# Two causal attentions of a fused kernel: two tiles per elementwise instruction, doubled buffers, a query transpose in another PSUM bank

## The reference, cut to what matters

```
layer 0: q, k = elu(.) + 1;  S_t = S_{t-1} + k_t v_t^T;  z_t = z_{t-1} + k_t
         y_t = (q_t S_t) / (q_t . z_t + 1e-6);  x += gate * (y @ w_proj)
layer 1: q, k rotated (rope), decay folded into the tables
         o_t = q_t sum_{s<=t} k_s v_s^T;  y = group_norm(o) * w + b
         x += gate * ((silu(h Wg^T) * y) @ Wo^T)
```

## Time and profile before

| | |
|---|---|
| runs (us) | 1041.17, 1035.74, 1040.65; median 1040.65 |
| span of the profiled execution | 1034.5 us, 25463 instructions |
| its time around the span | not listed apart; the three runs are 1.2 to 6.7 us over the span |
| busy, share of the span | PE 83%, PEld 59%, DVE 83%, ACT 61%, POOL 71% |
| mean granted TensorE clock | 0.937 |
| layer 0's attention, first to last products | 48.7 to 294.7 us |
| layer 1's attention, first to last products | 391.6 to 663.0 us |

### The profile page before, as it was taken

How to read it: one execution, slowest core, us unless ns; L and a number is a source line. 1 busy time by engine, 2 the same in 40 slices (tenths; PEclk the granted TensorE clock), 3 DMA queues, 4 the chain that set the end, 5 groups by cost and what they waited for, 6 DMA issues and landing times. The chain is left out here.

```text
span 1034.5 us, 25463 instructions
## 1 busy us (share of the span) xinstructions
PE 855.4 (83%) x5240; PEld 612.9 (59%) x5240; DVE 859.7 (83%) x2837; ACT 629.3 (61%) x1652; POOL 736.5 (71%) x642
## 2 busy tenths in 40 slices
PE   5699999999969968989898989558888733999993
PEld 4466666666636745555555555335655533999993
DVE  5589999999977976989888889778899861899995
ACT  2655555555429946676767675467765203998992
POOL 4488888888854528999999999655598471355554
PEclk9899999999989979999999999969999755999997
DMA  9520000000000000000000000264567564544420
GB/s 247 172 63 1 0 0 0 0 0 0 1 4 1 1 0 1 11 21 10 20 10 20 10 20 10 59 162 108 167 208 214 185 223 125 151 132 133 134 64 21
DMA packets 64935, 70.11 MB, mean 68 GB/s; under 512 B 8965, under 2 KB 52178, under 8 KB 64740
## 3 DMA queue, kind: packets, MB, share of 16 engines
q1 hardware_dynamic: 50612, 47.20, 16.5%
q0 software_dynamic: 6368, 16.89, 4.8%
q10 hardware_dynamic: 7872, 5.08, 2.0%
HBM read 32.32 MB, written 24.50 MB: 55 GB/s over the span
## 5 line engine op out<-in xcount | busy, mean ns | idle before, releaser
L473 PE MATMUL a_pS<-a_kv,utri 128*128 128x360 f32 (+3 forms) x768 | 263.1, 479 | 17.6 <-POOL a_kv L464 7.2
L464 POOL TENSOR_TENSOR a_kv<-a_qk,a_vv 128x1152 f32<-128x1152 f32 (+1 forms) x128 | 263.9, 2063 | 13.3 <-DVE a_qk L438 13.3
L473 PEld LDWEIGHTS a_pS<-a_kv,utri 128*128 128x128 f32 x768 | 135.5, 190 | 98.8 <-issue 24.6
L569 POOL TENSOR_TENSOR a_tt<-a_tt 128x576 f32<-128x576 f32 (+1 forms) x128 | 156.7, 1225 | 48.2 <-DVE a_tt L553 44.3
L553 DVE TENSOR_TENSOR a_tt<-a_pS,a_qk 128x360 f32<-128x360 f32 (+3 forms) x384 | 180.8, 526 | 9.1 <-PE a_pS L473 6.3
L1950 POOL DMA_INDIRECT out_dram<-x_o,x_place x71 | 69.4, 977 | 75.9 <-DVE x_o L1937 71.4
L581 DVE TENSOR_REDUCE a_nd<-a_tt 128x144 f32<-128x720 f32 (+3 forms) x128 | 104.3, 815 | 0.0
L519 ACT ACTIVATE a_tt<-a_pI 128x144 f32<-128x144 f32 (+1 forms) x96 | 40.1, 417 | 105.3 <-PE a_pI L481 105.2
L512 PEld LDWEIGHTS a_pO<-wgate,a_yT 128*128 128x128 f32 x256 | 44.6, 192 | 75.7 <-issue 42.5
L1530 POOL DMA_INDIRECT ys<-m_S,m_dest x64 | 62.9, 984 | 33.5 <-issue 12.5
L512 PE MATMUL a_pO<-wgate,a_yT 128*128 (+1 forms) x256 | 54.5, 295 | 31.5 <-POOL a_yT L543 22.6
(11 more groups left out here) (299 smaller groups left out, 2187.5 us busy)
## 6 DMA issues: line engine op xcount, KB each, us to landing
x_yl<-ys SPq DMA_DIRECT2D x71, 193.5 KB, 2.5
X<-xs SPq DMA_DIRECT2D x16, 256.0 KB, 5.3
kx<-m_kc SPq DMA_DIRECT2D x64, 64.0 KB
ax<-m_pc SPq DMA_DIRECT2D x64, 64.0 KB
m_S<-X SPq DMA_DIRECT2D x16, 256.0 KB, 4.4
xs<-X SPq DMA_DIRECT2D x15, 256.0 KB
w<-in_L_ffn_W_dram SPq DMA_DIRECT2D x1, 2048.0 KB
m_S<-gw ACTq DMA_DIRECT2D x6, 256.0 KB, 3.2
```

The lines of the kernel that those rows point to most:

```text
L464: pool.tensor_tensor(kv[:, t % 2, :, :, :], kk.unsqueeze(2).to_broadcast([P, H, J, D]), vv[:, t, :, :].unsqueeze(3).to_broadcast([P, H, J, ...
L473: pe.matmul(pS[c][:, 0:(h1 - h0) * SC], K.utri[:, :], flat[:, h0 * SC:h1 * SC], start=True, stop=True).then_inc(u_done, 1)
L569: pool.tensor_tensor(tt[:, t % 2, :, :, D // 2:D], tt[:, t % 2, :, :, D // 2:D], tt[:, t % 2, :, :, 0:D // 2], ALU.add).then_inc(half_done, 1)
```

## The change

The following is done for a pair of tiles (2u, 2u+1) in one instruction: kv, rope add, halving, gate product, denominator, reciprocal, y, its copy, square, variance, square root, residual. The three products, the sums, the state, the values' copy, exp and vec_qk stay per tile. kv and tt have four tiles instead of two. The query transpose moves from bank pI to columns 384 to 511 of the query bank pQ. `sum`, `y` and the rest now lag by one, two, three pairs. ScalarE loads the square root's table right after the silu. VectorE's short steps stand between the three products. Cut to its core:

```diff
-        qk = sb("qk", [P, TPB, 2 * P])
+        qk = sb("qk", [P, 2, TPB, P])
-        kv = sb("kv", [P, 2, H, J, D])
-        tt = sb("tt", [P, 2, H, J, D + 1])
+        kv = sb("kv", [P, TPB, H, J, D])
+        tt = sb("tt", [P, TPB, H, J, D + 1])
...
 def pe_qkv:
                 wait(pe, v_ready, m)
                 wait(pe, qk_free, m)
+                wait(pe, qT_ready, 3 * b - 3 + t)
...
+        def pool_kv(pool, b, u):
+            n, t = 2 * b + u, 2 * u
+            pool.wait_ge(qk_ready, qk_count(b, t + 1))
+            pool.wait_ge(v_ready, 4 * b + t + 2)
+            wait(pool, u_done, 6 * (n - 1))
...
+        def pe_transpose_q(pe, b, t):
+            m = 4 * b + 4 + t - 1
+            if isinstance(b, int):
+                m = min(m, NT)
+            pe.wait_ge(v_ready, m)
+            pe.wait_ge(qk_ready, qk_count(b, t))
+            pe.wait_ge(qk_free, m)
+            wait(pe, qT_ready, 3 * b + t - 1)
+            pe.transpose(pQ[:, QT:QT + P], qk[:, 0, t, :], K.ident[:, :]).then_inc(q_T, 1)
...
 def act_qT:
             act.wait_ge(q_T, 3 * b + t)
+            if known(b, 1):
+                act.wait_ge(qkv_ps, 4 * b + 4 + t)
...
 def act_gate:
+            act.activation(gate[slot], pT[:, :], ACT.Silu).then_inc(gate_ready, 1)
+            act.preload_act_table_set("sqrt_and_others")
...
+        def pe_step(pe, b, u, first=False):
+            ta, tb = 2 * u, 2 * u + 1
+            cur, back, out = pair(b, u, 0), pair(b, u, -2), pair(b, u, -3)
+            if cur and not first:
+                pe_states(pe, b, ta)
+            if out:
+                pe_project(pe, *out)
+            if cur:
+                if ta > 0:
+                    pe_inter(pe, b, ta)
+                pe_state_sum(pe, b, ta)
+                pe_transpose_q(pe, b, ta + 1)
+                if known(b, 1):
+                    pe_qkv(pe, b + 1, ta)
+            if back:
+                pe_transpose_y(pe, back, b, u)
+            if cur:
+                if layer == 1 and u == 0 and known(b, 1):
+                    pe_gate(pe, b + 1)
+                pe_states(pe, b, tb)
+                pe_inter(pe, b, tb)
+                if tb < 3:
+                    pe_state_sum(pe, b, tb)
+                    pe_transpose_q(pe, b, tb + 1)
+                if known(b, 1):
+                    pe_qkv(pe, b + 1, tb)
+                if u == 1 and known(b, 2):
                     pe_transpose_x(pe, b + 2)
...
+        def vec_step(v, b, u):
+            ta, tb = 2 * u, 2 * u + 1
+            cur, last, out, done = pair(b, u, 0), pair(b, u, -1), pair(b, u, -3), pair(b, u, -4)
+            late = last and known(last[0], 1) and (last[0] + 1, 2 * last[1] + 1)
+            if cur:
+                vec_product(v, b, ta, 0)
+            if layer == 0 and done:
+                vec_stats(v, *done, 0)
+            if layer == 1 and late:
+                vec_qk(v, *late)
+            if cur:
+                vec_product(v, b, ta, 1)
+            if layer == 0 and late:
+                vec_qk(v, *late)
+            if out:
+                vec_residual(v, *out)
+            if cur:
+                vec_product(v, b, ta, 2)
+            if last:
+                vec_sum(v, last[0], 2 * last[1])
+            if cur:
+                vec_state(v, b, ta)
+            if last:
+                vec_sum(v, last[0], 2 * last[1] + 1)
+            if cur:
+                vec_product(v, b, tb, 0)
+            if layer == 0 and last:
+                vec_den(v, *last)
+            if cur:
+                vec_product(v, b, tb, 1)
+                if known(b, 1):
+                    vec_qk(v, b + 1, ta)
+            if last:
+                if layer == 0:
+                    vec_rec(v, *last)
+                else:
+                    vec_var(v, *last)
+            if layer == 0 and done:
+                vec_stats(v, *done, 1)
+            if cur:
+                vec_product(v, b, tb, 2)
+                if tb < 3:
+                    vec_state(v, b, tb)
+            if last:
                 if layer == 1:
...
+                    vec_rec(v, *last)
+                vec_y(v, *last)
...
+        def pool_step(pool, b, u, phase):
+            last, back, ahead = pair(b, u, -1), pair(b, u, -2), pair(b, u, 1)
+            if last:
+                pool_halve(pool, *last)
+            if ahead:
                 if layer == 1:
+                    pool_rope(pool, *ahead)
+                pool_kv(pool, *ahead)
+            if layer == 1 and back:
+                pool_gate(pool, *back, (phase - 1) % 3)
```

More of the change, by code:

```diff
@@ L298, in attention @@
     SC = D * J
+    NP = NT // 2
     heads = [(0, 6), (6, 11), (11, 16)]
@@ L515, in act_inter, with pe_project @@
+        def pe_project(pe, b, u):
+            n = 2 * b + u
+            pe.wait_ge(yT_ready, n + 1)
+            wait(pe, x_done, n)
+            pe.wait_ge(y_ready, min(n + 2, NP) if isinstance(b, int) else n + 2)
+            for k in range(2):
+                mm = pe.matmul(pO[:, k * P:(k + 1) * P], yT[:, k, :], tile(K.wgate[:, 0 if layer == 0 else 2, :, :], b),
+                               start=True, stop=True)
+            mm.then_inc(proj_ps, 1)
         def act_inter(act, b, t):
@@ L663, in act_batch @@
-        def act_batch(act, b, half, last=False, more=True):
-            for t in range(TPB):
-                if t == 0 and not last:
+        def pe_step(pe, b, u, first=False):
[25 more added lines that the diff above has]
+                if u == 1 and known(b, 2):
+                    pe_transpose_x(pe, b + 2)
@@ L673, in act_batch @@
-                if layer == 1 and near(b, t, -1):
-                    act_square(act, *near(b, t, -1))
-                if t < 3:
-                    act_qT(act, b, t + 1)
-                if near(b, t, -2):
-                    act_yT(act, *near(b, t, -2))
-                if layer == 5 and t == 3 and more:
-                    act_modulate(act, b + 2)
-                if layer == 1:
-                    if near(b, t, -1):
-                        act_sd(act, *near(b, t, -1))
-                    if t == 2 and not last:
-                        act_gate(act, b + 1, 1 - half)
@@ L713, in pool_batch @@
-        def pool_batch(pool, b, half, last=False):
-            for t in range(TPB):
-                if not (last and t == 3):
-                    pool_kv(pool, 4 * b + t + 1, (t + 1) % 4)
-                if layer == 1:
-                    if near(b, t, -3):
-                        pool_gate(pool, *near(b, t, -3), half if t == 3 else 1 - half)
-                    if near(b, t, 3):
-                        pool_rope(pool, *near(b, t, 3))
-                pool_halve(pool, b, t)
+                    act_normalise(act, b + 2, ta)
@@ new lines, in act_step @@
+                act_qT(act, b, ta + 1)
+                if known(b, 1):
+                    act_qkv(act, b + 1, ta)
+            if back:
+                act_yT(act, *back)
+            if layer == 1 and last:
+                act_square(act, *last)
+            if cur:
+                act_inter(act, b, tb)
+                if more:
+                    act_normalise(act, b + 2, tb)
+            if layer == 1 and last:
+                act_sd(act, *last)
+            if cur:
+                if tb < 3:
+                    act_qT(act, b, tb + 1)
+                if known(b, 1):
+                    act_qkv(act, b + 1, tb)
+                if layer == 1 and u == 0 and known(b, 1):
+                    act_gate(act, b + 1, (phase + 1) % 3)
```

398 lines of the change are left out of this document (179 added, 219 removed).

## The result

The changed kernel takes 1054.82 us (median of 4 runs, 1050.93 to 1055.68) against 1040.91 for the kernel before: a ratio of 1.0145 [1.0119, 1.0171], slower by 13.9 us where 28 less were forecast. The profiled execution took 1054.64 us around a span of 1052.8.

A forecast was written before the change was run, and what follows sets the result against it. DVE bounds layer 0 and POOL layer 1; after the change, bank pQ's ring (7.5 us a pair) and POOL (7.68). Layer 1's -22.8 and layer 0's -5 take the 1034.5 us span to 1006.7, median 1013, range 995 to 1031.

The forecast's parts named there:

- signs of being wrong: What would refute the forecast: layer 1's period over 7.9 us a pair with POOL idle, or layer 0's over 7.8.
- The ring through bank pQ: Loop in each pair: DVE's qk reads bank pQ, PE projects, next states, first product; forecast 7.5 us a pair.
- Layer 1's ring: The same loop through bank pQ in layer 1, put at 7.5 us a pair, under POOL's 7.68.
- The early table load at nothing: Layer 1, square root's table loaded after the silu: delay on ACT put at no cost, 0.7 us a batch if uncovered.
- Layer 1's total: POOL bounds layer 1 at 7.68 us a pair; 244.1 against 272.7 us, -28.6, or -22.8 with the drain.
- Rival A: Rival, chance 0.1: POOL's time goes with the elements alone, so merging saves no fixed part; 17.4 us come back, 1030.
- Layer 0's total: Layer 0 at 7.5 us a pair: 240.8 against 247.4 us, -6.6, or -5 with the drain.
- The drain of layer 1: Statistics after layer 1's last products come 5.8 us later (+3 to +7); bank pO waits for the last pair's y.
- Layer 0's fill: Layer 0's first product comes 2.9 us later, since the first kv covers two tiles.
- C: Rival, chance 0.1: query transpose and its ACT copy lengthen bank pQ turns; zero gain at 0.52 us a pair, 1058 at 0.8.
- D: Rival, chance 0.08: the early table load does not help, sd is late again; 11 us, giving 1024.
- B: Rival, chance 0.2: layer 0's bank pQ loop is shorter, POOL's ring or PE bounds at 7.2 or less; 1003 to 995.

The follow-up runs named there:

- run 7: Changed kernel with the residual behind the third product of the pair's first tile instead of ahead of it; 1048.6 us, ratio 1.009 to the kernel before.
- Run 6: Changed kernel with PE's gate matmul of layer 1 behind the second tile's states instead of ahead of them; 1047.5 us.
- run 3: Kernel before with only the early table load added, the square root's table loaded right after the silu; 1051.9 us, ratio 1.012.
- run 9: Run 1 with the other qk step (next batch's second tile) also moved ahead of the first tile's first product; 1018.7 us.
- run 10: Run 9 with a tile's three products in a row again and the short steps behind them; 1016.5 us.
- run 13: Run 1 with each layer's first kv in two instructions and the last pair's reciprocal in bank pQ, its residual order changed for the drain; 1014.4 us.
- run 5: Run 1 without the early table load behind the silu; 1032.3 us.
- run 11: Changed kernel with a tile's three products in a row, so each qk step stands behind all three; 1125.8 us.
- run 1: Changed kernel with qk of the next batch's first tile ahead of the second tile's first product instead of after its second; 1027.4 us.
- run 4: Changed kernel without the early table load; 1051.5 us, ratio 1.011 to the kernel before.
- run 8: Changed kernel with the first tile's qk moved half as far, ahead of the second tile's second product but behind its first; 1032.9 us.
- Run 2: Kernel before with only the query transpose moved to bank pQ, with the changed kernel's waits; 1039.2 us, ratio 0.999.
- run 12: Run 1 with each layer's first kv in two instructions, layer 1's reciprocal in SBUF and an earlier residual at the drain; 1025.0 us.

## Why the prediction was wrong

Both of its signs of being wrong came: layer 1's period over 7.9 with POOL idle, and layer 0's over 7.8.

**The ring through bank pQ** is the step that failed. The prediction drew it rightly ("The new tie is bank pQ") and put it at 7.5 us in both layers, where 8.0 and 8.5 were measured. In layer 0, in two consecutive pairs (the step that the prediction calls odd is the one shown above, the even one runs from 101.92 to 109.88):

| link | forecast odd, even | measured odd, even |
|---|---|---|
| step's start to the first tile's qk | 5.03, 5.18 | 5.30, 5.47 |
| qk to PE (transpose of q in even steps) | 0.48 | 0.51, 0.51 |
| PE until the states start | 1.08, 0.77 | 1.20, 1.06 |
| states' start to first product | 1.03 | 1.03, 0.92 |
| pair | 7.62, 7.46 | 8.04, 7.96 |

One piece has a name and comes in every pair: the residual's wait for the projection, 0.19 to 0.22, which I had left out as if pO were always ready; run 7 got 0.23 a pair for it. The rest are small pieces of up to 0.2, of which the projection is the one that comes in both steps: 0.72 and 0.75 us until the next instruction starts, 0.64 forecast. A sum of bare durations leaves such pieces out, and the ring came 7% over it.

**Layer 1's ring** was waved through with "the same, 7.5". It was 8.4 and 8.6. On it stand two waits that weren't counted, one in each pair of a batch. From the timeline of the changed kernel:

```profile
505.15 0.41 PE L521 MATMUL a_pI<-ident,a_y 128*128 128x128 f32 x2 [0.86 <-ACT a_tt L538]
506.24 1.03 DVE L574 TENSOR_TENSOR a_tt<-a_pS,a_qk 128x384 f32<-128x384 f32 x2 [0.74 <-PE a_pS L485]
...
513.17 1.02 PE L670 MATMUL a_pT<-a_hT,W 128*128 128x512 f32 x2
514.88 1.03 DVE L574 TENSOR_TENSOR a_tt<-a_pS,a_qk 128x384 f32<-128x384 f32 x2 [0.40 <-PE a_pS L485]
```

In one pair DVE waits 0.74 for the second tile's states, which stand behind the transpose of y and so behind the table loads; in the other it waits 0.40 for them behind the gate matmul (0.86 us, once a batch). Without these two waits both pairs, 8.71 and 8.38, would be at 7.98, as far over the forecast as layer 0's. Run 6 took the second away, 7.6 us or 0.5 a batch.

**The early table load at nothing** rested on a cover: "PE's last projection waits for a later DVE step anyway". That projection was not where the delay went. It went to the transpose of y and to the states behind it in PE's queue (0.81 us on ACT's copy in the changed kernel, 1.37 in run 3), ahead of the wait that was to hide it. The price named for a failed cover was 0.7 a batch. Run 3 lost 0.46 in a batch by the chain, and 0.8 on average over 15 with what came with the clock.

**Layer 1's total** (-29.7 for the products, -5.2 measured): with the rings out of the way (runs 9 and 10) POOL does set the period, as forecast, at 7.90 instead of 7.68. That term was mis-sized by 0.22, and not in the merges: the records shrank by 0.77 a pair, less four overlaps of 0.05, which is the forecast 0.56. What it left out is kv's new wait of 0.16 for the rope add, in place of an overlap of 0.05. Rival A did not come: the fixed part was the instruction's. The prediction had read the Trainium skill (Advanced Engine Details and Errata, The Read-Write Bubble) as saying that nothing would be saved. That page says only that the bubble between instructions doesn't affect GpSimd; a fixed part inside the instruction, as in the 7.85 us of records against 8.62, it doesn't speak of.

**Layer 0's total** (-9.5, +5.4 measured): the pQ ring at 8.0. What lies beneath it is near the prediction's other terms: run 9's pairs are 7.4 on average, against PE's 7.1 and POOL's 7.2. Which of them bounds there no run asked.

**Fill and drain.** The drain of layer 1 was right, +5.9 for +5.8 (its sum, 7.0 less 1.3, gives 5.7), and for the named reason, as run 13 shows by removing it. Layer 0's fill was 2.0 dearer than forecast. In the timeline of PE after:

```profile
51.72 2.41 PE L485 MATMUL a_pS<-a_kv,utri 128*128 128x432 f32 x3 [4.13 <-POOL a_kv L475]
```

Three of the first states' matmuls took 2.41 us, where elsewhere all six take 2.10, behind 4.13 us of idling for the doubled kv, and the first product came 1.84 behind their start. The windows of the changed kernel and, second, of the kernel before over its first states:

```profile
50.85:57.68 6.83, 5.79 (x14) 3.44 (x14) 1.98 (x4) 0.86 (x2) 4.93 (x2) 0.50 1.03 284
47.66:48.69 1.03, 1.03 (x3) 0.68 (x4) 0.35 (x1) 1.03 (x4) 1.03 (x1) 1.00 1.05 354
```

The granted clock fell to 0.50 (1.2 of 2.4 GHz) while PE idled and stayed there until 57.68. Before, it was 1.00 over these states, and the product came after 1.03; so it was in run 13, whose clock did not fall. That is 0.8 of the 2.0. The other 1.2 is no cost of the change: the very first qk, ahead of the first changed step, starts at 46.12 instead of 44.93, and anywhere from 45.0 to 47.6 in the fourteen runs. From it to the first states it is 5.60 us instead of 2.73, 2.9 more, as forecast.

Between the layers 3.9 us more than forecast were lost. From the last product to the FFN's first statistics step it is 3.0 more than before instead of 1.6. The FFN, whose code is unchanged, took 2.4 more (before, then after):

```profile
303.86:377.12 73.26, 62.74 (x391) 46.48 (x391) 60.30 (x152) 61.49 (x132) 34.59 (x36) 0.94 0.01 2
317.10:392.79 75.69, 65.75 (x391) 49.13 (x391) 60.38 (x152) 61.44 (x132) 34.59 (x36) 0.91 0.01 2
```

This goes with the granted clock: in runs 5, 10 and 11 the FFN took 75.7 us at a mean clock of 0.88, in runs 1, 4 and 6 to 9 it took 73.2 to 73.9 at 0.94 to 0.97. So these 2.4 us come and go from one execution to the next. What makes the clock fall there no run asked.

**The rivals.** C named the size: zero at 0.52 us a pair over the forecast, and it was 0.5 in layer 0 and 0.8 in layer 1. Its cause, the query transpose and its copy inside the bank's turn, is not what the trace shows: where a wait of PE ahead of its writes to bank pQ names an engine, in layer 0's steady pairs it is DVE and never ACT, and the steps with the transpose are the shorter ones. Run 2 fits that, but in a kernel with time in hand. A chance of 0.1 for it was too small: with 0.15 in hand in layer 1 and a ring added up from bare durations, the ring being the longer one was the likelier case. D was right that the early load does not help, for another reason. B's shorter period exists, at 7.4, but only once both qk steps are moved.

## What to carry to other kernels

Where one bank passes from TensorE to VectorE and back once a step, write the ring down link by link, including every instruction queued ahead on both engines in their order, and add a margin; a sum of bare durations is its lower bound. Then look at the place of the reading instruction before anything else: one step moved by 1.1 us past two products was worth 27 us here. Merged instructions make each handoff coarser, which is paid at fill and drain, and can be undone for the first and last pair alone.

## What the runs showed of the hardware

**VectorE and GpSimd hold each other up when VectorE reads two operands from SBUF.** With the reciprocal in PSUM, y takes 0.420 us, the halving 2.147 and the gate product 0.727 (means of 23 in run 13, layer 1). With it in SBUF (run 12) they take 0.676, 2.232 and 0.816 (means of 22 or 23). In the rows of run 12 above, y starts at 443.38 within the gate product, ends 0.28 after it, and the halving that follows at once is 0.19 longer than its usual 2.14. The groups, of run 13 and of run 12:

```profile
L650 DVE TENSOR_TENSOR a_y<-a_nd,a_pO 128x256 f32<-128x256 f32 x23 | 9.7, 420 | 0.8
```

```profile
L645 DVE TENSOR_TENSOR a_y<-a_nd,a_rec 128x256 f32<-128x256 f32 x23 | 15.5, 676 | 0.8
```

The extra is the meeting's and not the operand's: the last y of run 12, at 653.29, with no GpSimd instruction beside it, takes 0.43. The first one shows the most, from the timeline of run 12:

```profile
401.88 2.13 POOL L592 TENSOR_TENSOR a_tt<-a_tt 128x1024 f32<-128x1024 f32 x1
402.18 2.11 DVE L645 TENSOR_TENSOR a_y<-a_nd,a_rec 128x256 f32<-128x256 f32 x1
```

The halving was first and keeps its 2.13; y takes 2.11 in place of 0.43 and ends 0.28 after it. The Trainium skill (SBUF — State Buffer, SBUF: two separate sides) says that a VectorE instruction with two SBUF inputs and a GpSimd instruction that reads SBUF share a pair of ports: the one that starts first has it for its whole length, and the other stands still. These rows agree with it.

**An engine's busy share is not its floor.** TensorE was busy for 237.7 us of layer 0's products in the changed kernel, 233.5 in run 1 and 228.0 in run 9, with the same 978 records. The projection's matmul, the one that waits for qk, shows a part of it: 531, 511 and 504 ns on average in the three. Another part is the clock, which was at 0.50 for 4.1 us of this stretch in the changed kernel and for 4.2 in run 1, but for 1.6 in run 9.

**The granted clock is part of a comparison.** In layer 1's products the changed kernel spent no time at clock 0.50 and run 1 spent 7.2 us. The last batch of layer 1 took 14.9 us in run 1, with 3.4 of them at 0.50, and 13.2 in run 13, with none.
